# Latent cross-attentions: the context block's value product in the layout of the other value products

## The reference, cut to what matters

```
q = lat @ Wq;  kv = concatenate([x, lat]) @ Wkv;  k, v = split(kv)    # x: 64 context rows, lat: 512 rows
attn = softmax(q k^T * scale)                                        # 512 queries x (64 + 512) keys
out = attn @ v;  result = concatenate(out of all heads) @ Wout
```

## Time and profile before

| | us |
|---|---|
| timed runs, median of 3 (lowest to highest) | 3958.56 (3958.35 to 3964.81) |
| profiled execution, its own time | 3928.34 |
| its span, first to last instruction | 3926.0 |
| TensorE matmuls busy | 3483.6 |
| VectorE busy | 2189.6 |
| ScalarE busy | 1495.9 |
| GpSimd busy | 1371.7 |
| mean granted TensorE clock (share of full) | 0.931 |

### The profile page before, as it was taken

How to read it: one execution, slowest core, us unless ns; L and a number is a source line. 1 busy time by engine, 2 the same in 40 slices (tenths; PEclk the granted TensorE clock), 3 DMA queues, 4 the chain that set the end, 5 groups by cost and what they waited for, 6 DMA issues and landing times. The chain is left out here.

```text
span 3926.0 us, 54458 instructions
## 1 busy us (share of the span) xinstructions
PE 3483.6 (89%) x18930; PEld 2234.7 (57%) x18930; DVE 2189.6 (56%) x5367; ACT 1495.9 (38%) x3039; POOL 1371.7 (35%) x1904
## 2 busy tenths in 40 slices
PE   7998897899999977789798999998996779996997
PEld 5675684445555567344444555555893445554896
DVE  5374444646556567666366676765334356665454
ACT  2253112434434364233244444443451144442553
POOL 2141441423223245233254444533422144442311
PEclk9999978999999988899799999999898789997998
DMA  2004001000000000000100000001321000003212
GB/s 101 1 1 124 14 1 46 1 1 1 1 1 1 13 1 8 17 1 1 49 1 1 1 1 1 1 1 50 135 76 52 0 29 1 1 1 160 72 60 84
DMA packets 48718, 108.85 MB, mean 28 GB/s; under 512 B 6660, under 2 KB 32900, under 8 KB 46404
## 3 DMA queue, kind: packets, MB, share of 16 engines
q1 hardware_dynamic: 40964, 84.88, 6.4%
q0 software_dynamic: 7488, 20.49, 1.5%
HBM read 70.67 MB, written 34.68 MB: 27 GB/s over the span
## 5 line engine op out<-in xcount | busy, mean ns | idle before, releaser
L2653 POOL TENSOR_SCALAR probs<-probs,inv_sum 128x512 f32<-128x512 f32 x640 | 438.2, 698 | 1007.1 <-DVE inv_sum L2774 1006.8
L2616 ACT ACTIVATE probs<-psum_banks,neg_max 128x576 f32<-128x576 f32 x640 | 468.6, 737 | 743.3 <-DVE neg_max L2857 743.3
L2857 DVE TENSOR_REDUCE neg_max<-psum_banks 128x1 f32<-128x576 f32 x640 | 454.7, 752 | 213.5 <-PE psum_banks L2491 206.9
L2491 PE MATMUL psum_banks<-keys_T,queries_T 64*128 64x288 f32 x2560 | 406.8, 437 | 52.5 <-ACT probs L2616 43.2
L2783 DVE COPY probs_T<-psum_banks 128x512 f32<-128x512 f32 x640 | 408.7, 679 | 4.0 <-PE psum_banks L2411 4.0
L2491 PEld LDWEIGHTS psum_banks<-keys_T,queries_T 64*128 64x128 f32 x2560 | 224.8, 189 | 269.6 <-ACT probs L2616 148.4
L2411 PE MATMUL psum_banks<-ident,probs 128*128 128x128 f32 x2560 | 357.4, 283 | 3.2 <-POOL probs L2653 2.3
L2411 PEld LDWEIGHTS psum_banks<-ident,probs 128*128 128x128 f32 x2560 | 281.2, 143 | 128.9 <-POOL probs L2653 64.8
L2441 PE MATMUL psum_banks<-probs_T,values 128*64 128x512 f32 x1280 | 309.3, 605 | 2.2 <-issue 2.2
L4406 PE MATMUL psum_banks<-sorted_T,tile_weights 128*128 128x128 f32 x2208 | 266.2, 278 | 4.9 <-ACT tile_weights L4496 4.9
L4406 PEld LDWEIGHTS psum_banks<-sorted_T,tile_weights 128*128 128x128 f32 x2208 | 258.5, 195 | 5.7 <-issue 5.6
(11 more groups left out here) (534 smaller groups left out, 6119.2 us busy)
## 6 DMA issues: line engine op xcount, KB each, us to landing
normed<-sorted_rows SPq DMA_DIRECT2D x30, 385.5 KB, 3.3
sorted_rows<-zero_rows SPq DMA_DIRECT2D x8, 1028.0 KB, 14.6
w_L_experts_down<-in_L_experts_down SPq DMA_DIRECT2D x2, 4096.0 KB, 31.2
normed<-expert_outputs SPq DMA_DIRECT2D x8, 1024.0 KB, 6.9
w_L_xattn_Wkv<-in_L_xattn_Wkv SPq DMA_DIRECT2D x2, 2048.0 KB, 8.1
w_L_experts_up<-in_L_experts_up SPq DMA_DIRECT2D x1, 4096.0 KB, 12.9
sorted_rows<-zero_rows SPq DMA_DIRECT2D x4, 899.5 KB, 14.5
x_res<-in_x SPq DMA_DIRECT2D x4, 512.0 KB, 7.0
```

The costliest lines, as they stand in the source:

```text
L2491: last = pe.matmul(k.ps[:, 2 * h + a, 0:HALF], qT[r, b % 2, j, t * P:(t + 1) * P], kT[r, j, k0:k0 + HALF], start=True, stop=True)
L2616: act.activation(prob[:, g % PB, h * w:(h + 1) * w].rearrange("p (a n) -> p a n", a=2), k.ps[:, 2 * h:2 * h + 2, 0:HALF], ACT.Exp, bias=nm ...
L2653: pool.tensor_scalar(w, w, inv[:, g % 4, h:h + 1], 1.0, ALU.mult, ALU.mult).then_inc(shared, 1)
L2857: dve.tensor_reduce(nmax[:, g % 4, h:h + 1], k.ps[:, 2 * h:2 * h + 2, 0:HALF], AX.XY, ALU.max, negate=True).then_inc(maxed, 1)
```

## The change

The context values get a second copy's worth of room: `context_values` is [128, 2, pairs, 64] instead of [128, pairs, 64], with an index for the head. Head h's values stay on partitions 64h to 64h + 63 of its part; the other 64 partitions of that part are filled with zeros, once a stage, by two VectorE instructions placed ahead of the wait for the context rows. The product of the context block takes all 128 partitions for each head: the partitions that hold the other head's keys meet zeros. TensorE waits for the fills before its first such product.

```diff
-        vc = k.sb("context_values", [P, PAIRS, NC], st)
+        vc = k.sb("context_values", [P, 2, PAIRS, NC], st)
...
                         pe.wait_ge(ctx_value_moved, b * A + j // 4 + 1)
+                        if q == 0:
+                            pe.wait_ge(zeroed, 2)
                     for c in ((0, 1), (2, 3, 4))[part]:
                         for h in range(2):
                             r = slice(64 * h, 64 * h + 64)
...
-                                last = pe.matmul(k.ps[r, 6, :], vc[r, j, :], pTc[r, q % 2, :], start=False, stop=True)
+                                last = pe.matmul(k.ps[r, 6, :], vc[:, h, j, :], pTc[:, q % 2, :], start=False, stop=True)
...
-                            act.copy(vc[r, 4 * a:4 * a + 4, :], k.ps[r, 7, :].rearrange(
+                            act.copy(vc[r, h, 4 * a:4 * a + 4, :], k.ps[r, 7, :].rearrange(
                                 "p (j s d) -> p j s d", s=2, d=64)[:, :, h, :]).then_inc(sem, 1)
...
                 batch_aggr(0)
+                for h in range(2):
+                    dve.memset(vc[64 - 64 * h:128 - 64 * h, h, :, :], 0.0).then_inc(zeroed, 1)
                 dve.wait_ge(ctx_loaded, 16)
```

More of the change, by code:

```diff
@@ L2267, in latent_attention @@
         with signals(nc, "ctx_stat", "ctx_aggr", "ctx_shift", "ctx_rstd", "ctx_normed", "ctx_turned", "ctx_ready",
-                     "ctx_loaded", "mask_made", "stats", "aggr", "shift", "rstd", "normed", "norm_turned", "norm_moved",
+                     "ctx_loaded", "mask_made", "zeroed", "stats", "aggr", "shift", "rstd", "normed", "norm_turned", "norm_moved",
                      "made", "act_moved", "dve_moved", "squared", "summed", "floored", "inverted", "scaled", "turned",
                      "moved", "placed") as (
-                ctx_stat, ctx_aggr, ctx_shift, ctx_rstd, ctx_normed, ctx_turned, ctx_ready, ctx_loaded, mask_made, stats, aggr,
+                ctx_stat, ctx_aggr, ctx_shift, ctx_rstd, ctx_normed, ctx_turned, ctx_ready, ctx_loaded, mask_made, zeroed, stats, aggr,
                 shift, rstd, normed, norm_turned, norm_moved, made, act_moved, dve_moved, squared, summed, floored,
```

## The result

The changed kernel took 3950.6 us in the median of 20 runs (3943.74 to 3958.17), beside 3961.28 us (3954.34 to 3965.04) for 20 runs of the kernel before on the same chip. The ratio is 0.9975 (95% interval 0.9968 to 0.9981), so -9.9 us (-12.7 to -7.5). The forecast was -11.8 us, 0.30% less. Run again on another occasion, beside other runs of the kernel before, the same program had 0.9971 (0.9959 to 0.9983).

What follows compares the result with a forecast made beforehand. TensorE's own list was taken to bound the steps holding the context product. 79 savings of 0.15 us, with fills and wait at 0, gave 3958.56 - 11.8 = 3946.8 us, range 3939 to 3956.

Steps and rivals of the forecast that it cites:

- What bounds the step: Loop over score tiles: TensorE's own work sets the length of steps holding the context product, at least 1.09 us in hand.
- TensorE's list: TensorE's own work in a loop step, context product last; predicted to set that step's length.
- the ring: Loop over score tiles: scores on TensorE, maximum on VectorE, exponential on ScalarE, then next scores; can set other steps' length.
- The sign named for it: Scores L2491: TensorE's wait for ScalarE's exponential should stay as it is.
- The cost of the product: Context product L2444: 1.01 us falls to 0.86, dropping 0.09 for a layout change and 0.05 for a first slot.
- 65 places: Those of the 80 context products that are followed by scores; each predicted to gain the full 0.15 us.
- The weight loads: Context product's new 128-row loads: predicted hidden beside the preceding slot's matmuls, as the value slots' loads are.
- The rival: Context product: exposed loads cost 0.14 us per slot, +10.6 us, or heads run one after the other, +57; chance 0.03.
- The fills: Two VectorE zero fills per stage: 0.33 to 1.62 us for both, hidden by the 1.87 us load wait; cost 0.
- Where the saving goes: Three cross-attention stages: 79 of 80 products keep 0.15 us, 11.8 in all; by layer 4.8, 4.8 and 2.25.
- The one product counted as lost: Layer 3, before the last transposes: its 0.15 us is lost because TensorE waits 2.29 us for GpSimd's scaling.
- the batch changes: Granted-clock rival: one more 1.2 GHz stretch at each of 9 gaps between batches loses 13 to 16 us; chance 0.03.
- The sum: Whole kernel: -11.8 us in the loops, 0 for fills and wait, giving 3946.8 us, 0.30% less.

Runs made afterwards that it cites:

- experiment 2: Kernel before, with the context block's two old 64x64 matmuls moved between value blocks 2 and 3; ratio 1.0053 (1.0039 to 1.0066), +20.8 us.
- experiment 3: Changed kernel with the context block's new product moved between value blocks 2 and 3; ratio 0.9986 (0.9977 to 0.9995) to the kernel before, -5.5 us.
- experiment 4: Changed kernel with both heads' context values in one 128x128 operand, one matmul in place of two; ratio 1.0011 (1.0002 to 1.0019) to the kernel before.
- Experiment 1: Changed kernel's room, fills and wait kept, but the product is the old two 64x64 matmuls; ratio 0.9998 (0.9989 to 1.0008) to the kernel before.
- experiment 7: Kernel before plus a 1024-element VectorE fill at the end of layer 1's cross-attention, delaying what follows; ratio 1.0010 (0.9999 to 1.0022).
- experiment 5: The changed kernel unaltered, run again beside other runs of the kernel before; ratio 0.9971 (0.9959 to 0.9983), -11.5 us.
- experiment 6: Changed kernel with 10 of 80 context products moved behind the next step's transposes as one 128x128 matmul; ratio 0.9954 (0.9940 to 0.9967) to the kernel before.
- experiment 8: Kernel before plus VectorE fills of 3520 elements at the end of layer 1's cross-attention, a longer delay; ratio 1.0015 (1.0005 to 1.0024).

## Why the prediction was right

*What bounds the step.* Right. With the saving the scores behind the product still started when TensorE reached them; the last exponential had ended 0.95 us earlier in the masked stages (1.09 before), so the shorter step took all of it from TensorE's list and none from the ring. The sign named for it holds: TensorE's wait for ScalarE ahead of the scores did not grow (191.6 us).

*The cost of the product.* Right in both terms: 0.09 for the change of layout and 0.05 for the first slot, 0.147 us by the unrounded starts against 0.15 predicted, at every one of the 65 places; experiments 2 to 4 show that the layout is the cause, and neither the 64 rows nor the place. The Trainium skill, TensorEngine Tiling (Array Packing), Key Properties, says that switching the tiling mode drains the engine. The traces agree, in that the last slot ahead of a switch takes 0.53 us instead of 0.43 and the loads behind it come only with the next slot, and they put a price on it: 0.15 us for a visit.

*The weight loads.* The rival failed. The rule of the Trainium skill (TensorE: Matmul & The Clock Gate, Part 3) that loads overlap running matmuls only across row groups does not hold for these operands: loads of 128 rows start 0.43 us apart beside matmuls of 128 rows, and the 0.14 us never shows. The heads stayed side by side: four records in 1.03 us, each 592 ns.

*The fills.* Right: 0.48 us each in layers 1 and 2, so 0.97 for both, between the bounds of 0.33 and 1.62, and hidden. Experiment 1 has no difference.

*Where the saving goes.* Right for layer 1 (-4.7 and -4.5 of 4.8), near for layer 2 (-4.2 and -4.3 of 4.8), wrong in size for layer 3 in both profiles (0 of 2.25). The one product counted as lost was lost: TensorE's wait for GpSimd grew from 2.29 to 2.44 us, the 0.15 saved ahead of it. What is missing is the granted clock. I had put its loss at the batch changes and thought single stretches of 2 or 3 us either way likelier than the loss of the whole gain, and such a stretch is what the two traces have; it came at the stage's end, beside the wait for GpSimd that I had read. It is not owed to the new product alone: of ten traces the last value products have slow slots in five, two with the old product (experiments 1 and 7, layer 3's stage 440.58 and 442.10 us) and three with the new one (the changed kernel twice, experiment 3). In those two traces four slots are slow, in the changed kernel's seven.

*The sum.* -11.8 was forecast, -9.9 (-12.7 to -7.5) measured and -11.5 (-16 to -7) the second time; the new product in the middle of the accumulation gave -5.5 (-9.0 to -2.0). In the profiles 8.9 us are kept in the three stages. That each product gives 0.147 us at its place is shown; that the whole kernel keeps all 11.8 is neither shown nor excluded.

For every timed execution of experiments 1 to 8 the mean granted clock is on record, and it tells where the misses lie. "By places" is what the starts at the product's place give (for experiment 6 with its 8.6 us, for 7 and 8 the measured delay), "timed" what the ratio gives, in us; the clock is the mean over the runs, less that of the kernel before beside them.

| experiment | by places | timed | timed - by places | clock |
|---|---|---|---|---|
| 1, fills only | 0 | -0.8 | -0.8 | 0.0000 |
| 2, between, old product | +11.8 | +20.8 | +9.0 | -0.0030 |
| 3, between, new product | -11.8 | -5.5 | +6.3 | -0.0018 |
| 4, one square matmul | +2.8 | +4.3 | +1.5 | -0.0008 |
| 5, the change again | -11.8 | -11.5 | +0.3 | -0.0008 |
| 6, free step | -20.4 | -18.2 | +2.2 | -0.0007 |
| 7, short delay | +1.2 | +4.0 | +2.8 | -0.0020 |
| 8, long delay | +3.1 | +5.9 | +2.8 | -0.0009 |

The two misses that are clear of the intervals, experiments 2 and 3, come with two of the three largest drops of the clock, one with the old product and one with the new; experiment 1 has neither a miss nor a lower clock. As an estimate, a mean lower by 0.0030 over 3950 us is 24 us more at 1.2 GHz instead of 2.4, which cost at most 12 us, and 0.0018 at most 7: enough for the 9.0 and the 6.3. So the saving at the place is the predicted one, and in the two clear cases what the total is off by goes with the clock. What gives one kernel a lower clock than another is not shown.

## What to carry to other kernels

Count TensorE's changes of layout along its list as a cost of their own, some 0.15 us a visit here, and fill an operand with zeros to the layout of its neighbours where that adds no slot. Put a product whose layout can be chosen beside work of the same layout, and into a step that another engine bounds. Judge a change of 0.3% by the starts at its own place and by stage lengths first, and by the total only beside the clocks of the timed runs: whole profiles differed by 23 us the wrong way.

## What the runs showed of the hardware

Three things I had not expected. A first slot behind a change of layout was 0.05 us longer for a 128-column operand than for 64-column ones (2.92 against 2.87); that the size of its load is the reason is likely and not tested. The way out of a product costs nothing where the work behind it has its layout: 2.83 us in experiment 4 where 128x128 work follows, 2.92 where the scores do. And stages that no edit touches came out at one of two lengths, 377 or 383 us for layer 2's self-attention at a granted clock of 0.89 to 0.90 or 0.88, and 115 to 117 or 120 to 121 for layer 0's cross-attention, which runs ahead of every edit. What picks the one or the other I could not tell.
